# A centred, feature-major first norm for half the tokens in a cross-attention and expert layer

## Reference

```
x = x + block1(layernorm(x))    # 4 experts, all with weights ctx[e] (256 x 256), used three times:
                                # z = h @ ctx[e].T ; y = (silu(z) * z) @ ctx[e].T, expert by token id
x = x + block2(layernorm(x))    # 16 experts of width 96, 4 chosen by sigmoid router + bias,
                                # weights normalised, plus one shared expert of width 96
```

## Time and profile before

| | us |
|---|---|
| median of 3 executions | 170.04 (169.79 to 170.05) |
| the profiled execution | 170.02 |
| its span, first to last instruction | 167.8 |
| TensorE busy | 162.7 (97%) |
| VectorE busy | 114.9 (69%) |
| ScalarE busy | 68.6 (41%) |
| GpSimd busy | 37.6 (22%) |

### The profile page before, as it was taken

The page is one execution under the profiler, slowest core; times in us unless marked ns, Lnnn a source line. Parts: engine busy times, 40 slices in busy tenths (PEclk is TensorE's granted clock), DMA queues, the critical chain, the costliest instruction groups (busy, mean ns, idle before and its releaser), DMA issues.

```text
span 167.8 us, 2177 instructions
## 1 busy us (share of the span) xinstructions
PE 162.7 (97%) x703; PEld 128.7 (77%) x703; DVE 114.9 (69%) x237; ACT 68.6 (41%) x116; POOL 37.6 (22%) x36
## 2 busy tenths in 40 slices
PE   7899999999999999999999999999999999999992
PEld 2578888888787888888888877888888888888880
DVE  1899898756966998879996754867824444444452
ACT  3743442741349144436734528452222222222210
POOL 1393000566232035555960000000000000000000
PEclk9999999999999999999999999999999999999999
DMA  5991470064404066988225500035442221100003
GB/s 170 281 393 53 123 273 1 5 184 187 125 4 127 16 184 177 241 243 213 73 48 162 165 0 4 0 96 172 159 153 66 63 63 63 64 0 0 0 0 125
DMA packets 12198, 18.77 MB, mean 112 GB/s; under 512 B 3772, under 2 KB 6044, under 8 KB 12060
## 3 DMA queue, kind: packets, MB, share of 16 engines
q1 hardware_dynamic: 12188, 18.64, 36.3%
HBM read 16.39 MB, written 2.24 MB: 111 GB/s over the span
## 4 chain that ended last, share of the span: by engine, by line
PE 95%; DMA 2%; DVE 1%; issue 0%; DVEq 0%
PE bank L1027 23%; PE bank L1118 14%; PE bank L1117 13%; PE bank L1116 13%; PE bank L1136 7%; PE bank L1139 7%; PE bank L1137 7%; DMA first<-first_d 2%; PE bank L1055 1%; PE bank L1061 1%; PE bank L1068 1%; PE bank L1113 1%; PE bank L1112 1%; PE bank L983 1%; PE bank L994 1%; PE bank L1006 1%
## 5 line engine op out<-in xcount | busy, mean ns | idle before, releaser
L1118 PE MATMUL bank<-xn_lo,gu_hi 128*128 128x512 f32 (+1 forms) x104 | 41.1, 395 | 0.0
L1116 PE MATMUL bank<-xn_hi,gu_lo 128*128 128x512 f32 x96 | 38.0, 396 | 0.0
L1117 PE MATMUL bank<-xn_hi,gu_hi 128*128 128x512 f32 x96 | 38.0, 396 | 0.0
L595 ACT ACTIVATE h_hi<-hid 128x512 fp32r<-128x512 f32 (+1 forms) x26 | 16.4, 632 | 45.7 <-DVE hid L856 45.7
L861 DVE TENSOR_TENSOR h_lo<-hid,h_hi 128x512 fp32r<-128x512 f32 (+1 forms) x26 | 17.9, 690 | 14.9 <-ACT h_hi L595 14.9
L1118 PEld LDWEIGHTS bank<-xn_lo,gu_hi 128*128 128x128 f32 (+1 forms) x104 | 19.4, 187 | 4.9
L585 ACT ACTIVATE act_sb<-bank 128x512 f32<-128x512 f32 (+1 forms) x26 | 15.4, 591 | 17.5 <-PE bank L1118 17.4
L468 POOL TENSOR_TENSOR gu_lo<-stage,gu_hi 128x512 fp32r<-128x512 f32 x12 | 17.2, 1458 | 21.8 <-ACT gu_hi L500 16.4
L1117 PEld LDWEIGHTS bank<-xn_hi,gu_hi 128*128 128x128 f32 x96 | 18.0, 188 | 4.4
L1116 PEld LDWEIGHTS bank<-xn_hi,gu_lo 128*128 128x128 f32 x96 | 18.0, 188 | 4.3
L745 DVE COPY_PREDICATED prod<-beyond,bank 128x512 f32<-128x512 uint8 x24 | 17.6, 739 | 5.3 <-PE bank L1027 4.7
(11 more groups left out here) (100 smaller groups left out, 214.8 us busy)
## 6 DMA issues: line engine op xcount, KB each, us to landing
stage<-gu_d SPq DMA_DIRECT2D x6, 512.0 KB, 3.6
stage<-wd_d SPq DMA_DIRECT2D x3, 512.0 KB, 4.4
first<-comb_d SPq DMA_DIRECT2D x8, 192.0 KB, 2.7
ids<-comb_d SPq DMA_DIRECT2D x8, 192.0 KB, 3.1
stage<-ctx_d SPq DMA_DIRECT2D x4, 256.0 KB, 5.4
xt<-xt_d SPq DMA_DIRECT2D x1, 1024.0 KB, 10.1
first<-comb_d SPq DMA_DIRECT2D x8, 128.0 KB, 2.9
ids<-comb_d SPq DMA_DIRECT2D x8, 128.0 KB, 2.9
```

The costliest lines, as they stand in the source:

```text
L1116: nc.tensor.matmul(out[:], gu_lo[:, cols], xn_hi[:, h, k], start=(k == 0), stop=False)
L1117: nc.tensor.matmul(out[:], gu_hi[:, cols], xn_hi[:, h, k], start=False, stop=False)
L1118: ins = nc.tensor.matmul(out[0:rows, :], gu_hi[:, wide], xn_lo[:, h, k], start=False, stop=(k == KC - 1))
```

## The change

Half 1's first norm isn't made on tokens any more. VectorE takes the statistics, transposes the moments, and SP writes them to DRAM and reads the means back as a row to all partitions (`mean_all`). `subtract_means` subtracts that row from feature-major `xt`, into the place of token-major x, and `x_high` and `x_low` read from there. The eight transposes, `apply_norm(1)` and `layer_norm_apply(1)` go. 1/deviation of both halves takes one power on GpSimd, one transpose, one write and one read (512 KB), and is applied to the picked product in all four mixes of layer 1. The load of `xt` is split: half 1 early, half 0 behind the rows. A ctx piece now holds two experts of one output block; x of half 1 is loaded between the second and third, and `first_mix` takes the experts in pairs. The x1 transposes move into expert 1 of mix 5, behind its first feature; picks, norm and Silu around them change places.

```diff
-    pieces = [("ctx", e * KC * D, KC * D) for e in range(E1)]
+    pieces = [("ctx", n * CTX, CTX) for n in range(KC * E1 // 2)]
...
+        ctx_hi = sb("ctx_hi", [P, KC, E1, KC, P], F32R)
+        ctx_lo = sb("ctx_lo", [P, KC, E1, KC, P], F32R)
...
+        side_order = [
+("x1", 0, 0, 4), ("x1", 0, 1, 5), ("n2", 0, 0, 4), ("n2", 0, 1, 5)]
...
+            if (what, h) == ("n1", 1):
+                return x[:, TT:].rearrange("p t d -> p (t d)").rearrange("p (k c) -> p k c", k=KC)[:, k]
...
-                e = at // (KC * D)
-                st = st.rearrange("p (k f) -> p k f", k=KC)
-                return ctx_d[:, e], st, ctx_hi[:, e], ctx_lo[:, e]
+                m, pair = at // CTX // (E1 // 2), at // CTX % (E1 // 2)
+                hi, lo = (w[:, m, 2 * pair:2 * pair + 2].rearrange("p e k f -> p (e k f)") for w in (ctx_hi, ctx_lo))
+                return ctx_d[:, at:at + cols], st, hi, lo
...
             sp.dma_start(first[:, P + PAIR:P + 2 * PAIR], x_d[:, 0:PAIR]).then_inc(x_in[1], 16)
             load_piece(0)
-            for n in range(1, SLOTS):
+            load_piece(1)
+            sp.dma_start(first[:, P + 2 * PAIR:], x_d[:, PAIR:]).then_inc(x_in[2], 16)
+            for n in range(2, SLOTS):
                 load_piece(n)
-            sp.dma_start(first[:, P + 2 * PAIR:], x_d[:, PAIR:]).then_inc(x_in[2], 16)
             sp.dma_start(ids[:], ids_d.partition_broadcast(P)).then_inc(ids_in, 16)
-            sp.dma_start(xt[:], xt_d).then_inc(xt_in, 16)
+            sp.dma_start(xt[:, :, HALF:], xt_d[:, :, HALF:]).then_inc(half_in, 16)
             sp.dma_start(bias[:], bias_d.partition_broadcast(P)).then_inc(bias_in, 16)
+            sp.wait_ge(moments_turned, 1)
+            sp.dma_start(moments_d.rearrange("t (q i) -> q t i", i=LANES), moments_row[:]).then_inc(moments_out, 16)
+            sp.wait_ge(moments_out, 16)
+            sp.dma_start(mean_all[:].rearrange("p (t c) -> p t c", c=P),
+                         moments_d.rearrange("(t two) c -> two t c", two=2)[0, 0:TT].partition_broadcast(P)).then_inc(mean_in, 16)
             sp.wait_ge(deviation_turned, 1)
             sp.dma_start(rstd_d.rearrange("t (q i) -> q t i", i=LANES), deviation_row[:]).then_inc(rstd_out, 16)
             sp.wait_ge(rstd_out, 16)
-            sp.dma_start(rstd_all[:], rstd_d[0:TT].rearrange("t c -> (t c)").partition_broadcast(P)).then_inc(rstd_in, 16)
+            sp.dma_start(rstd_all[:].rearrange("p h c -> p (h c)"),
+                         rstd_d[0:HALVES * TT].rearrange("t c -> (t c)").partition_broadcast(P)).then_inc(rstd_in, 16)
             sp.wait_ge(rstd_in, 16)
+            sp.dma_start(xt[:, :, 0:HALF], xt_d[:, :, 0:HALF]).then_inc(xt_in, 16)
             for n in range(SLOTS, len(pieces) - 2):
...
+            def first_deviations():
+
+                pool.wait_ge(varied, HALVES)
+                nc.gpsimd.tensor_tensor(deviation[:, 0:HALVES * TT], vareps[:, 0:HALVES].rearrange("p n t -> p (n t)"),
+                                        power[:], ALU.pow).then_inc(powered, 1)
...
-            for n in range(E1):
+            pool.wait_ge(deviation_zero, 2)
+            for n in range(E1 - 1):
                 low_part(n)
-            rstd_of(0)
-            rstd_of(1)
+            first_deviations()
+            low_part(E1 - 1)
...
-                if mixes[n][1] == 0:
-                    act.wait_ge(z_scaled, n + 1)
-                else:
-                    act.wait_ge(z_picked, (n + 1) * (E1 - 1))
+                act.wait_ge(z_scaled, first_layer.index(n) + 1)
...
             first_z(0)
-            apply_norm(1)
             first_z(1)
             x_high("n1", 1, 0)
...
             first_z(5)
+            apply_norm(2)
             silu_z(5)
-            apply_norm(2)
             x_high("n2", 0, 0)
             x_high("n2", 0, 1)
             first_z(6)
...
+            def turn_means():
+
+                dve.wait_ge(dstep, steps[0])
+                dve.wait_ge(deviation_zero, 2)
+                for t in range(TT):
+                    step(nc.vector.bn_aggr(moments[:, 2 * t:2 * t + 2], stats[:, t]))
+                dve.wait_ge(dstep, steps[0])
+                nc.vector.transpose(moments_row[:], moments[:]).then_inc(moments_turned, 1)
...
+            def subtract_means(k):
+
+                dve.wait_ge(mean_in, 16)
+                dve.wait_ge(half_in, 16)
+                nc.vector.tensor_tensor(features("n1", 1, k), xt[:, k, HALF:], mean_all[:], ALU.subtract).then_inc(centred, 1)
...
 
                 dve.wait_ge(rstd_in, 16)
                 dve.wait_ge(z_picked, (n + 1) * (E1 - 1))
-                nc.vector.tensor_tensor(prod[:, n % 2], prod[:, n % 2], rstd_all[:], ALU.mult).then_inc(z_scaled, 1)
+                nc.vector.tensor_tensor(prod[:, n % 2], prod[:, n % 2], rstd_all[:, mixes[n][1]], ALU.mult).then_inc(z_scaled, 1)
...
                 _, h, m = mixes[n]
-                dve.wait_ge(xt_in, 16)
+                dve.wait_ge(half_in if h else xt_in, 16)
...
 
...
             dve.wait_ge(x_in[2], 16)
             for t in range(TT):
                 tile_stats(1, t)
-            layer_norm_vars(1)
+            turn_means()
+            nc.vector.tensor_scalar(vareps[:, 1], moments[:, 0:2 * TT].rearrange("p (t two) -> p t two", two=2)[:, :, 1],
+                                    EPS, None, ALU.add).then_inc(varied, 1)
             masked = [thresholds(0)]
+            pick(0, masked[0], [1])
             turn_deviations()
-            pick(0, masked[0], [1])
-            layer_norm_apply(1)
             pick(0, masked[0], [2, 3])
             pick(1, masked[0], [1])
+            subtract_means(0)
+            subtract_means(1)
             x_low("n1", 1, 0)
             x_low("n1", 1, 1)
             pick(1, masked[0], [2])
...
             hidden_low(1)
             masked.append(thresholds(1))
             pick(2, masked[1])
+            scale(2)
             pick(3, masked[0], [1])
             hidden_product(2)
             pick(3, masked[0], [2])
...
             add_block_1(3)
             pick(4, masked[0])
             add_block_1(4)
-            pick(5, masked[1], [1])
             for t in range(TT):
                 tile_stats(2, t)
             layer_norm_vars(2)
-            pick(5, masked[1], [2, 3])
+            pick(5, masked[1], [1, 2])
             layer_norm_apply(2)
+            pick(5, masked[1], [3])
+            scale(5)
             hidden_product(5)
...
+                    if n == 1:
+                        pe.wait_ge(w_hi, ctx_piece(m, e) + 1)
+                        pe.wait_ge(w_lo, ctx_piece(m, e) + 1)
...
                             operands(k, True)
                         ins = term(e, k, 0, 1, stop=(k == KC - 1))
+                        if k < KC - 1 and e in within:
+                            within[e]()
...
                 z = [ring_bank("z", 0, e)[:] for e in range(E1)]
-                f = slice(0, P)
 
                 def high(e):
-                    pe.wait_ge(w_hi, e + 1)
+                    pe.wait_ge(w_hi, ctx_piece(0, e) + 1)
                     for k in range(KC):
-                        nc.tensor.matmul(z[e], ctx_hi[:, e, k, f], xn_hi[:, 0, k], start=(k == 0), stop=False)
-
-                def x_low(e, stop):
+                        nc.tensor.matmul(z[e], ctx_hi[:, 0, e, k], xn_hi[:, 0, k], start=(k == 0), stop=False)
+
+                def weights_low(e):
+                    pe.wait_ge(w_lo, ctx_piece(0, e) + 1)
+                    for k in range(KC):
+                        nc.tensor.matmul(z[e], ctx_lo[:, 0, e, k], xn_hi[:, 0, k], start=False, stop=False)
+
+                def x_low(e):
                     pe.wait_ge(pair_low, 1)
                     pe.wait_ge(xlo_done, KC)
                     for k in range(KC):
-                        ins = nc.tensor.matmul(z[e], ctx_hi[:, e, k, f], xn_lo[:, 0, k], start=False, stop=stop and k == KC - 1)
-                    if stop:
-                        ins.then_inc(z_done, 1)
-
-                def weights_low(e, stop):
-                    pe.wait_ge(w_lo, e + 1)
-                    for k in range(KC):
-                        ins = nc.tensor.matmul(z[e], ctx_lo[:, e, k, f], xn_hi[:, 0, k], start=False, stop=stop and k == KC - 1)
-                    if stop:
-                        ins.then_inc(z_done, 1)
+                        ins = nc.tensor.matmul(z[e], ctx_hi[:, 0, e, k], xn_lo[:, 0, k], start=False, stop=(k == KC - 1))
+                    ins.then_inc(z_done, 1)
 
                 pe.wait_ge(pair_high, 1)
                 pe.wait_ge(xhi_done, KC)
-                high(0)
-                weights_low(0, False)
-                x_low(0, True)
-                for e in range(1, E1):
-                    high(e)
-                    x_low(e, False)
-                    weights_low(e, True)
+                for pair in range(0, E1, 2):
+                    for step in (high, weights_low, x_low):
+                        for e in range(pair, pair + 2):
```

(58 more changed lines are left out.)

17 lines of the change are left out of this document (8 added, 9 removed).

## The result

The changed kernel takes 170.6 us in the median, the kernel before 170.05 beside it: a ratio of 1.0031 [1.0018, 1.0044], 0.5 us slower. One of its 22 executions took 231.49 us, at a granted clock of 0.662, and isn't compared with the others. Its profiled execution tells another story: 170.02 us with a span of 167.6, where the kernel before has 170.02 and 167.8. Only two of the changed kernel's executions were quicker than the profiled one; the spans of the 21 go from 167.5 to 168.8 us.

What follows compares the result with a forecast made beforehand. TensorE, 95% of the chain, was taken as the bound, with VectorE and two DRAM trips having to keep up. -1.14 + 0.4 + 0.7 + 0.1 = +0.06 us on 170.04 gave 170.1 us; range 169.3 to 171.0.

Steps and rivals of the forecast that it cites:

- the rows are late: Rival, slower: mean row at 18.0 or deviation row at 21.2 us, stall 1.0 instead of 0.4, 170.7 us; chance 0.15.
- The transposes, -0.87: TensorE, mix 1: half 1's eight transposes go, saving 0.87 us in full if no new wait appears.
- The pairs, -0.27: TensorE, first mix: expert pairs take turns, low parts are wanted later; 24 products take 5.60 us instead of 5.87.
- The mean row and the deviation row, +0.4: DRAM trips ahead of mixes 2 and 3: rows in at 17.3 and 20.3 us, stalling TensorE 0.4, ends 0 and 1.3.
- GpSimd is idle at that moment: Half 0's `vareps` meets no GpSimd instruction, so half 1's statistics start at about 9.7 us instead of 10.62.
- the 16.9 that I had put as a sign of error: Sign of error: the mean row landing before 16.9 us (or after 18) would show the prediction wrong.
- The 0.35 us for 512-byte pieces: Mean row's trip: allowance for 512-byte pieces and xt still moving, 0.35 us taken from between 0 and 1.0.
- The wait of mix 6, +0.7: TensorE waits at mix 6's second feature for VectorE, lengthened by mix 5's scale: 0.7 us, ends 0.4 and 0.9.
- GpSimd in VectorE's way, +0.1: Around 30 to 37 us GpSimd may hold up `add_block_1(4)` or the second norm's `vareps`: 0 to 1.2 us, 0.1 taken.
- An add of over 1 us: Sign of error: VectorE's add of mix 4 lasting over 1 us would show the prediction wrong.

Runs made afterwards that it cites:

- the pairs alone: Kernel before with only ctx pieces by expert pair and output block and the first mix in pairs; norm unchanged: 0.9964 [0.9951, 0.9976], 169.36 us for 169.96.
- its fellow: The kernel before run again, unedited, for a second trace: 1.0005 [0.9986, 1.0025]; its stages in the table sum to 41.07 us.
- the second measurement: The changed kernel run again, unedited, for a second trace and a firmer ratio: 1.0052 [1.0035, 1.0069], 170.84 us for 169.93; profiled span 168.9.

## Why the prediction was right or wrong

The time, 170.6, lies in the range, 0.5 above the forecast of 170.1, and near the rival "the rows are late" with its 170.7. Step by step:

- **The transposes, -0.87.** Right: 6.46 to 5.60.
- **The pairs, -0.27.** Undersized. It was read from one execution's 5.87; the two pairs of traces give -0.2 and -0.6, the timed runs of the pairs alone -0.6. That the first mix depends on when it starts and when pieces land wasn't in the sum.
- **The mean row and the deviation row, +0.4, ends 0 and 1.3.** The mechanism was right and the trip's length nearly so. From the start of the statistics to the data in SBUF: predicted 17.3 - 9.7 = 7.6 us for the mean row, measured 17.5 - 10.3 = 7.2; for the deviation row 10.6 predicted, 10.7 and 11.0 measured. What failed is the step "GpSimd is idle at that moment", from which the 9.7 came. It holds in the first trace (9.31) and not in the second (10.30), because it hangs on the landing of a ctx piece; then TensorE waits 1.5 us, over my upper end of 1.3. And the step had no term for the landing of x of half 1, which came between 8.6 and 10.3 us in the traces with this order of loads and set the start by itself in three of them. In the first the mean row was in at 13.42 + 3.1 = 16.5, ahead of the 16.9 that I had put as a sign of error. The 0.35 us for 512-byte pieces wasn't due there: 256 KB in such pieces landed in 3.1 us in both traces of the changed kernel.
- **The wait of mix 6, +0.7.** Right in place, link and size: the way from the n2 transposes to the gate went from 2.27 to 3.09, +0.82.
- **GpSimd in VectorE's way, +0.1.** Right in size, 0.13: `add_block_1(4)` took 1.08 us instead of 0.69, and the x1 transposes came 2.18 behind mix 5's start, not 2.10. An add of over 1 us was a sign of error by my own list, and it cost this little. The meeting that mattered was the other one, of half 0's `vareps` in the first norm, which I had ruled out.
- **Not in the sum:** the power of eight numbers ahead of the last ctx low part, 0.28 us in two traces.

With the terms measured in the table, which must add up to its sums, the first trace is -0.87 - 0.20 + 0 + 0.82 + 0.13 = -0.12 against -0.11 in the table, and the second against its fellow is -0.58 - 0.87 + 1.50 + 0.99 = +1.04, as 42.11 - 41.07. The timed ratios of +0.3 and +0.5% lie between these two. Taken by parts, the pairs bring -0.36% and the norm costs 1.0031 / 0.9964 = +0.67%, 1.1 us (1.5 by the second measurement), though it takes 0.87 us of work from the engine that bounds the kernel. So part of the hit is luck: the rows cost 0 in one trace and 1.5 in the other, not 0.4, the pairs bring more than I took, and near effects of opposite sign made a forecast of no change look better than its working was.

What stays open: why the same load lands earlier in one execution than in another, and how often the late case comes, by GpSimd or by x. Two traces of the changed kernel show one of each; the timed spans say only that most lie above the first.

## What to carry to other kernels

A profile is one execution. Where a new wait ends on a load, a margin of 0.05 to 0.4 us is none: price it with the load late by what it differs between traces, back to the load that the trip starts from. Look, too, for tiny instructions that stand ahead of the start of a long trip and that another engine can hold up; moving this one away brought the start back to 9.27 in its trace, though its timed gain alone isn't shown. Work taken from the engine that bounds the kernel is a gain only if the engine that feeds it isn't given more on the way to the next thing that is wanted: here 0.87 us came off TensorE, and one scale of 0.69 us on VectorE came back as 0.83 us at mix 6. And group loads so that the first consumer needs as few of them as it can; the pairs were the part worth keeping.

## What the runs showed of the hardware

- The same 512 KB load of x, behind the same loads, landed 6.0 to 7.7 us after its issue over the traces with the changed kernel's order, and the ctx pieces (256 KB) 5.4 to 7.4 in the median of four over all traces.
- A broadcast of 256 KB from DRAM in 512-byte pieces landed in 3.1 us in both traces of the changed kernel and in 3.1 to 3.5 over all, one in 2 KB pieces in 3.1; 512 KB took 3.3 to 3.8.
- A 16 KB write to DRAM took 2.0 us alone, 2.6 to 2.7 when issued 0.4 to 0.7 us behind such a broadcast, and 2.0 to 2.1 when issued 1.0 to 1.4 us behind it.
- A VectorE `tensor_scalar` of four numbers a partition, 0.17 us by itself, took 0.69 to 1.25 us where a GpSimd instruction was under way, and ended 0.02 to 0.03 us after it in the seven traces in which both have a row of their own.
- GpSimd's power on 128 partitions: four numbers each 1.0 to 1.4 us, eight 1.75 to 1.9.
